# Layer normalisation of four parts placed in the part ahead, piece by piece, in a one-core four-layer network

## The chip, the cores and the metric

The kernel runs on one core of one Trainium2 chip. The metric is the device time of one execution in microseconds (us). Five engines matter: TensorE (PE in the rows; PEld is its loading of weights), VectorE (DVE), ScalarE (ACT), GpSimd (POOL) and SyncE (SP), which here only issues DMA. A name with a small q behind it, such as SPq, is an engine's instruction queue, where it issues transfers and waits.

## What is computed

A residual network over 2048 tokens of 128 features. Every one of its eight parts sees the layer normalisation of the running sum and adds onto it:

```python
    x = x + _L0_attn_ref(_layernorm(x, axis=-1), ...)   # mamba with its own feed-forward
    x = x + _L0_ffn_ref(_layernorm(x, axis=-1), ...)    # mixture of 8 experts, top 2
    x = x + _L1_attn_ref(_layernorm(x, axis=-1), ...)   # linear attention
    x = x + _L1_ffn_ref(_layernorm(x, axis=-1), ...)    # mixture of 8 experts, top 2, gated
    x = x + _L2_attn_ref(_layernorm(x, axis=-1), ...)   # causal attention with a decay by distance
    x = x + _L2_ffn_ref(_layernorm(x, axis=-1), ...)    # 8 experts of three layers, all computed
    x = x + _L3_attn_ref(_layernorm(x, axis=-1), ...)   # attention in a window of 64 tokens, rotary
    x = x + _L3_ffn_ref(_layernorm(x, axis=-1), ...)    # last feed-forward
```

with

```python
def _layernorm(x, axis=-1, eps=1e-05):
    m = jnp.mean(x, axis=axis, keepdims=True)
    v = jnp.var(x, axis=axis, keepdims=True)
    return (x - m) / jnp.sqrt(v + eps)
```

The decay attention subtracts |i - j| from the score of query i and key j, so far keys vanish:

```python
        scores = jnp.where(causal[None, None], -jnp.inf, scores) + decay[None, None]
        attn = jax.nn.softmax(scores, axis=-1)
        ...
        return out @ Wo.T + bo
```

## The kernel before

The running sum X stays in SBUF as 16 tiles of 128 tokens (T = 16), grouped into 4 chunks of 4 tiles (C = 4, CT = 4, CW = 512 tokens). The parts run one after the other, each a block with a program for each engine; between parts all engines meet. In the order of time they are mamba, experts (moe0), linear attention, experts (moe1), the decay mixer, deep (the eight experts of three layers), the window mixer, and the last feed-forward. Deep, the window mixer and the last feed-forward stand in one block.

Layer normalisation is five pieces, which class Norm (L198 to L251) provides for a chunk or for several at once (a sweep), and functions of class Core (L127 to L192) for linear attention: **stats** on VectorE (mean and variance of every tile, then the variance plus epsilon in veps), **power** on GpSimd (veps to the power of -0.5, in rstd), **rows** on VectorE (X less mean, times rstd, in xn or in rows), **turn** on TensorE (four transposes into a bank of PSUM) and **take** on ScalarE (the bank into xnT, which the projections read). Counting semaphores (ln_ve, ln_rs, ln_xn, ln_tr, ln_ev) order them across all parts.

The order of the work on each engine is the order in which it is written. Both mixers are one function, softmax_mixer (L2244). Its loop runs over y from FIRST = -2 to T + 1, with eight steps w = 0 to 7 in each (a step is two heads of sixteen); at one y TensorE makes the scores of tile y + 2 for the maxima (first_pass), those of tile y for the weights (second_pass), and the values, while VectorE takes the maxima of tile y + 2 (L2549) and adds the finished tile y - 2 onto X (add, L2623, at w = 1). GpSimd splits the queries and keys of the tiles from 2 on into parts of 16 bits (split, lines L2778 to L2785) and, in the decay mixer, computes their lengths (L2559 to L2566). There, X plus the output bias stands in a tile of its own, X0, written by one instruction:

```python
                if y == 4 and not windowed:
                    nc.gpsimd.tensor_tensor(X0[:], k.X[:], bo[:, None, :].to_broadcast([P, T, P]), ALU.add)\
                        .then_inc(s_x0, 1)
```

The decay mixer looks only at keys in a band near the query. A block behind it (from L2735) takes the largest lengths and computes a flag that says whether the band is enough; if not, all_keys computes the attention again over all keys from X0. With the data of this kernel the flag says that it is.

In the experts, each tile of 128 routed tokens is fetched by a gather and its answer scattered; the tail (both, onto_x, L1580 to L1588) adds both answers of a token and adds them onto X, chunk by chunk as the transfers land. Deep (L1769) has 32 units, an expert and a chunk each; a step n of its loop holds first(n), second(n - 1) and the third layer of n - 2, and in its first steps the turn and the gate of a chunk. The last feed-forward brings its own normalisation into the window mixer's loop by the tables TURNS, STATS, ROWS and TAKES, whose keys are (y, w).

Of the kernel before, what the change touches and what calls it, by code (L numbers as in the profile page):

```python
# [33 lines left out]
P = 128  # L34
# [8 lines left out]
class Core:  # L43
# [82 lines left out]

    def norm_stats(self, h, X=None):  # L127
        v = self.nc.vector
        X = self.X if X is None else X
        tiles, done = self.sweeps[h], self.Q + h + 1  # L130
        for i in tiles:
            last = v.bn_stats(self.stats[:, i, :], X[:, i, :])
        last.then_inc(self.ln_st, 1)
        self.wait_alone(v, self.ln_st, done)
        for i in tiles:
            last = v.bn_aggr(self.meanvar[:, i, :], self.stats[:, i, :])
        last.then_inc(self.ln_mv, 1)
        v.wait_ge(self.ln_mv, done)
        part = slice(tiles[0], tiles[-1] + 1)
        v.tensor_scalar(self.veps[:, part], self.meanvar[:, part, 1], EPS, None, ALU.add).then_inc(self.ln_ve, 1)  # L140

    def norm_rows(self, L0, c, X=None, keep=None):
        v = self.nc.vector
        X = self.X if X is None else X
        if c < 2:
            v.wait_ge(self.ln_rs, self.Q + c + 1)
        if L0 + c >= 2 and keep is None:
            v.wait_ge(self.ln_tr, L0 + c - 1)
        for i in range(CT):
            n = c * CT + i  # L150
            dst = self.xn[:, (L0 + c) % 2, i, :] if keep is None else keep[:, n, 0:P]
            last = v.tensor_scalar(dst, X[:, n, :], self.meanvar[:, n, 0:1],
                                   self.rstd[:, n:n + 1], ALU.subtract, ALU.mult)
        last.then_inc(self.ln_xn, 1)

    def norm_vector(self, L0, X=None, keep=None):
        for h in range(len(self.sweeps)):
            self.norm_stats(h, X)
        for c in range(self.C):
            self.norm_rows(L0, c, X, keep)  # L160

    def norm_pow(self, h):
        tiles = self.sweeps[h]
        part = slice(tiles[0], tiles[-1] + 1)
        self.nc.gpsimd.tensor_tensor(self.rstd[:, part], self.veps[:, part], self.mhalf[:, part], ALU.pow)\
            .then_inc(self.ln_rs, 1)

    def norm_pool(self):

        for h in range(len(self.sweeps)):  # L170
# [3154 lines left out]
```

## Time and profile before

| what | value |
|---|---|
| median of 3 runs | 1403.57 us (1401.08 to 1407.66) |
| profiled execution | 1401.1 us, span 1399.4 us |
| mean granted clock of TensorE | 0.909 |
| TensorE busy | 1105.9 us, 79% |
| VectorE busy | 892.5 us, 64% |
| ScalarE busy | 680.1 us, 49% |
| GpSimd busy | 573.1 us, 41% |
| instructions | 25149 |

The time is that of the whole execution; the span runs from the profile's first to its last instruction. The parts lie about so in the span: mamba to 344 us, experts to 497, linear attention to 538, experts to 724, decay mixer to 930, deep to 1055, window mixer to 1239, last feed-forward to the end. The granted clock is TensorE's, as a share of 2.4 GHz; 0.50 is 1.2 GHz. A profile holds one execution, and its time stands 2.5 us under the median of the runs.

### The profile page before, as it was taken

How to read it: one execution, taken by the hardware profiler on the slowest of the kernel's cores; microseconds unless marked ns; L12 is line 12 of the kernel's file. 1: busy time of each engine (PE TensorE's matmuls, PEld its weight loads, DVE VectorE, ACT ScalarE, POOL GpSimd, SP SyncE). 2: the span in 40 equal slices, each digit the busy share in tenths (PEclk: the TensorE clock that was granted, in tenths of full speed). 3: DMA queues.
4: the chain of work that ended last, by engine and by line, in shares of the span. 5: the costliest groups of instructions: out<-in, count | busy, mean ns of one | idle time of the engine just before them, and what ended most of it. 6: DMA issues, size and time to landing. Idle time of an engine off the chain costs nothing. (4 is left out here: it accounts for less than half of the span.)

```text
span 1399.4 us, 25149 instructions
## 1 busy us (share of the span) xinstructions
PE 1105.9 (79%) x8340; PEld 714.4 (51%) x8349; DVE 892.5 (64%) x2981; ACT 680.1 (49%) x1256; POOL 573.1 (41%) x739
## 2 busy tenths in 40 slices
PE   8876777679278644299936999859995999899998
PEld 3322222227178633199934777634333777654545
DVE  3599899995545456377549888743858778850200
ACT  2685466545134301132216888627664888641221
POOL 6188889882734414544435434120013655110000
PEclk9989999999589955599968999979996999999999
DMA  2999000000522215311120000020002000000000
GB/s 61 161 191 167 0 0 1 0 0 9 182 61 58 69 38 206 70 42 46 33 72 1 2 3 3 2 57 1 1 0 85 3 3 2 3 1 0 15 0 15
DMA packets 80456, 58.31 MB, mean 42 GB/s; under 512 B 14043, under 2 KB 69221, under 8 KB 80326
## 3 DMA queue, kind: packets, MB, share of 16 engines
q1 hardware_dynamic: 74630, 45.20, 15.3%
q0 software_dynamic: 4544, 9.38, 1.8%
q10 hardware_dynamic: 1152, 2.10, 0.4%
q8 instruction: 70, 1.15, 0.3%
q14 instruction: 60, 0.49, 0.1%
HBM read 28.13 MB, written 28.52 MB: 40 GB/s over the span
## 5 line engine op out<-in xcount | busy, mean ns | idle before, releaser
L713 PE MATMUL bank<-hC,ident 128*128 128x512 f32 x256 | 132.7, 643 | 48.7 <-POOL hC L998 46.7
L998 POOL TENSOR_TENSOR hC<-h,Cs 128x1024 f32<-128x1024 f32 x64 | 150.8, 2356 | 49.8 <-DVE h L897 49.5
L897 DVE TENSOR_TENSOR_SCAN h<-bank,state,dBx 128x512 f32<-128x512 f32 x128 | 157.3, 1270 | 3.7 <-POOL dBx L991 1.7
L1381 POOL DMA_INDIRECT moe_answers<-moe_yw,moe_xg x78 | 84.3, 1081 | 128.6 <-DVE moe_yw L1558 69.7
L2549 DVE CUSTOM_DVE_ANT_0 decay_below<-bank,decay_q_mask 128x256 bf16<-128x256 f32 x256 | 97.2, 419 | 23.0 <-PE bank L2361 22.1
L713 PEld LDWEIGHTS bank<-hC,ident 128*128 128x128 f32 x256 | 46.0, 197 | 111.2 <-POOL hC L998 71.8
L2549 DVE CUSTOM_DVE_ANT_0 window_below<-bank,window_q_mask 128x192 bf16<-128x192 f32 x256 | 80.4, 353 | 29.5 <-PE bank L2361 27.9
L810 ACT ACTIVATE bank<-dt,A 128x512 f32<-128x512 f32 x128 | 83.2, 683 | 28.1 <-DVE h L897 27.1
L1452 PE MATMUL bank<-moe_xgT,moe_wac 128*128 128x128 f32 x624 | 87.4, 286 | 6.5 <-issue 4.1
L2489 ACT ACTIVATE decay_pb<-bank 128x512 f32<-128x512 f32 x128 | 76.2, 598 | 33.3 <-PE bank L2376 32.7
L1467 PE MATMUL bank<-moe_wd,moe_hT 128*128 x624 | 83.0, 277 | 5.7 <-DVE moe_hT L1545 2.7
L1452 PEld LDWEIGHTS bank<-moe_xgT,moe_wac 128*128 128x128 f32 x624 | 80.4, 202 | 7.4 <-issue 4.5
L1467 PEld LDWEIGHTS bank<-moe_wd,moe_hT 128*128 128x128 f32 x624 | 76.4, 194 | 6.5 <-issue 6.4
L2489 ACT ACTIVATE window_pb<-bank 128x384 f32<-128x384 f32 x128 | 62.3, 491 | 34.3 <-PE bank L2376 32.4
L3174 DVE TENSOR_TENSOR f_ys<-bank,f_s 128x256 f32<-128x256 f32 x8 | 3.4, 424 | 117.4 <-PE bank L3117 117.4
L1254 POOL DMA_INDIRECT moe_slots<-moe_rows,moe_slot x64 | 62.3, 973 | 31.7 <-issue 16.6
L226 POOL TENSOR_TENSOR rstd<-veps,mhalf 128x4 f32<-128x4 f32 (+1 forms) x12 | 14.8, 1237 | 145.9 <-DVE veps L220 145.9
L1394 ACT ACTIVATE moe_xgT<-bank 128x128 f32<-128x128 f32 x78 | 20.9, 268 | 97.4 <-PE bank L1445 97.4
L883 DVE TENSOR_TENSOR dBx<-dtx,bank 128x768 f32<-128x768 f32 (+1 forms) x64 | 65.9, 1030 | 1.7 <-ACT taps_w L815 1.3
L832 ACT ACTIVATE Cs<-bank 128x512 f32<-128x512 f32 x64 | 38.1, 596 | 44.2 <-POOL hC L998 35.9
L1445 PE MATMUL bank<-ident,moe_xg 128*128 128x128 f32 x78 | 22.6, 290 | 42.5 <-DMA moe_xg<-moe_slots 41.6
L3108 PE MATMUL bank<-f_hB,f_h2w 128*128 128x512 f32 x128 | 55.3, 592 | 0.0
(480 smaller groups left out, 2834.2 us busy)
## 6 DMA issues: line engine op xcount, KB each, us to landing
moe_slots<-blank SPq DMA_DIRECT2D x16, 1040.0 KB, 17.6
moe_xg<-moe_slots SPq DMA_DIRECT2D x78, 65.0 KB, 1.9
moe_wa<-in_moe_w SPq DMA_DIRECT2D x2, 2048.0 KB, 9.5
moe_back<-moe_answers SPq DMA_DIRECT2D x8, 256.0 KB, 5.6
moe_back<-moe_answers ACTq DMA_DIRECT2D x8, 256.0 KB, 5.7
moe_wu<-in_moe_wu SPq DMA_DIRECT2D x1, 2048.0 KB
deep_w<-in_deep_w SPq DMA_DIRECT2D x3, 512.0 KB
moe_answers<-moe_yw,moe_xg POOLq DMA_INDIRECT x78, 2.5
```

The lines of the kernel that those rows point to most:

```text
L713: last = nc.tensor.matmul(sum_bank(hh)[:], k.ident[:], hC[:, u % 2, hh, :], start=(n == 0), stop=(n == NS - 1))
L810: nc.scalar.activation(decay_bank(u, hh)[:], dt[:, hh, cols(c)], ACT.Exp, scale=A[:, hh, n:n + 1]).then_inc(q_dA, 1)
L883: v.tensor_tensor(dBx[:, u % 2, :, 0:w], dtx[:, :, c * CW:c * CW + w], b_bank[:, None, 0:w].to_broadcast([P, H, w]), ALU.mult).then_inc(q_ ...
L897: v.tensor_tensor_scan(h[:, u % 2, hh, :], decay_bank(u, hh)[:], dBx[:, u % 2, hh, :], state[:, n, hh:hh + 1], ALU.mult, ALU.add).then_inc ...
L998: g.tensor_tensor(hC[:, u % 2], h[:, u % 2], Cs[:, u % 2, None, :].to_broadcast([P, H, CW]), ALU.mult).then_inc(q_hC, 1)
L1254: k.nc.gpsimd.indirect_dma_start(k.slots[self.name], index, self.rows[j][:, i, :], None)\
L1381: nc.gpsimd.indirect_dma_start(answers, bass.IndirectOffsetOnAxis(index, 0), yw[:, i % NY, :], None)\
L1452: last = nc.tensor.matmul(bank[1 + i % 2][:, f * P:(f + 1) * P], wac[:, i % 2, f * P:(f + 1) * P], xgT[:, i % 2, :], start=True, stop=True)
L1467: last = nc.tensor.matmul(bank[6 + i % 2][:, 0:P], hT[:, i % NH, f, :], wd[:, one, f, :].rearrange("p o d -> p (o d)"), start=(f == 0), st ...
L2489: nc.scalar.activation(pb[:, w % 4, :], bank[2 + w % 2][:, 0:2 * HW], ACT.Exp).then_inc(s_ex, 1)
L2549: last = nc.vector.tensor_tensor_reduce(out=below[:, 2 * g + j, :], in0=bank[g % 2][:, j * HW:(j + 1) * HW], in1=q_mask[:], scale=-1.0, sc ...
L3108: last = k.nc.tensor.matmul(bank[4 + m % 4][:], self.hw[layer][:, i, f * P:(f + 1) * P], src[:, i, :], start=(i == 0), stop=(i == FB - 1))
```

## The change

It has six parts.

1. Norm serves linear attention as well, and the functions of Core go. There each chunk is a sweep of its own. Chunk 0's stats and power stand in the tail of the experts ahead (moe0).
2. In the decay mixer the sweeps are now (0), (1), (2, 3) where they were (0), (1, 2, 3). All five pieces of chunk 0 stand in the tail of moe1. stats(1) stands ahead of the loop, the stats of the sweep (2, 3) behind the maxima of (y, w) = (-2, 7), rows of chunk 2 at (-1, 3) and of chunk 3 at (0, 3). The window mixer has the same tables and sweeps, and its own chunk 0 where it was.
3. The normalisation of chunks 0 to 2 of deep stands in the decay mixer's loop, by the tables of the new class NormAhead, which also serves the last feed-forward, in new steps. Deep turns and normalises only chunk 3, computes three gates first, and waits for its weights one layer at a time. The turned rows of deep lie in another buffer (blank).
4. X0 becomes a copy of X, made at y = 6, and X gets the output bias in place by the instruction behind it. add reads X.
5. The check of the band stands in the decay mixer's loop, at y = 12 and 13, in place of the block behind it. The branch for all keys normalises again what it needs.
6. The table of tile ends in the experts is one scan in place of a copy and seven adds.

```diff
+class NormAhead:
+
+    STATS = {(11, 2): 0, (12, 2): 1, (14, 2): 2}
+    ROWS = {(13, 2): 0, (15, 2): 1, (15, 3): 2}
+    TURNS = {(14, 2): 0, (15, 4): 1, (16, 0): 2}
+    TAKES = {(14, 4): 0, (15, 6): 1, (16, 0): 2}
...
+    def vector_step(self, dve, y, w):
+        if (y, w) in self.STATS:
+            dve.wait_ge(self.added, (self.STATS[y, w] + 1) * CT)
+            self.norm.stats(dve, self.STATS[y, w])
+        if (y, w) in self.ROWS:
+            self.norm.rows(dve, self.ROWS[y, w])
+
+    def pool_end(self, pool):
+        for c in range(self.k.C - 1):
+            self.norm.power(pool, c)
...
@@ experts
-                step(v.tensor_copy(ends[:, 0:1], tiles[:, 0:1]))
-                for e in range(1, E):
-                    step(v.tensor_tensor(ends[:, e:e + 1], ends[:, e - 1:e], tiles[:, e:e + 1], ALU.add))
+                step(v.tensor_tensor_scan(ends[:], k.ones[:, 0:E], tiles[:], 0.0, ALU.mult, ALU.add))
...
                 both(0)
-                for c in range(C):
-                    if c + 1 < C:
-                        both(c + 1)
-                    onto_x(c)
+                onto_x(0)
+                dve.wait_ge(s_x, 1)
+                after.stats(dve, 0)
+                both(1)
+                onto_x(1)
+                if full:
+                    after.rows(dve, 0)
+                both(2)
+                both(3)
+                onto_x(2)
+                onto_x(3)
...
@@ linear
-                k.norm_vector(L0, keep=rows)
+                for c in range(C):
+                    norm.rows(dve, c, keep=rows)
+                    if c + 1 < C:
+                        norm.stats(dve, c + 1)
...
@@ deep, tensor
-            turn(0)
+            for c in range(C - 1):
+                gate(c)
             for n in range(STEPS):
                 if n < units:
                     first(n)
-                if n + 1 < C:
-                    turn(n + 1)
-                if 0 <= n - 1 < C:
-                    gate(n - 1)
+                if n == 0:
+                    turn(C - 1)
+                if n == 1:
+                    gate(C - 1)
...
@@ deep, scalar
-            take_turned(0)
-            act.wait_ge(w_1, 32)
-            act.wait_ge(w_2, 32)
-            act.wait_ge(w_3, 32)
+            for c in range(C - 1):
+                take_logits(c)
             for n in range(STEPS):
+                if n == 0:
+                    act.wait_ge(w_1, 32)
                 if n < units:
                     relu_first(n)
...
@@ softmax_mixer
+        FLAG_AT = T - 3
...
+        TURN_AT = {-2: 1, 0: 2, 1: 3}
+        ROWS_AT = {(-1, 3): 2, (0, 3): 3}
...
         def add(dve, y):
             dve.wait_ge(s_pr, y + 1)
-            base = k.X if windowed else X0
             if y == 0 and not windowed:
-                dve.wait_ge(s_x0, 1)
-            nc.vector.tensor_tensor(k.X[:, y, :], bank[7][:, P:2 * P], base[:, y, :], ALU.add).then_inc(s_x, 1)
+                dve.wait_ge(s_x0, 2)
+            nc.vector.tensor_tensor(k.X[:, y, :], bank[7][:, P:2 * P], k.X[:, y, :], ALU.add).then_inc(s_x, 1)
...
@@ vector
+            m.ready(dve)
             if not windowed:
-                for c in range(C):
-                    vector_head(dve, c)
-            m.ready(dve)
+                norm.stats(dve, 1)
...
-                if 1 <= y + 4 < C:
-                    norm.rows(dve, y + 4)
...
+                    if (y, w) == (FIRST, G - 1):
+                        norm.stats(dve, 2)
+                    if (y, w) in ROWS_AT:
+                        norm.rows(dve, ROWS_AT[y, w])
...
+                    if not windowed and (y, w) == (FLAG_AT - 1, 7):
+                        band_is_enough(dve, 0)
+                    if not windowed and y == FLAG_AT and w >= 4:
+                        band_is_enough(dve, w - 3)
...
@@ gpsimd
+            norm.power(pool, 1)
             for y in range(OWN, T):
+                if y == 4:
+                    norm.power(pool, 2)
...
-                if y == 4 and not windowed:
-                    nc.gpsimd.tensor_tensor(X0[:], k.X[:], bo[:, None, :].to_broadcast([P, T, P]), ALU.add)\
+                if y == 6 and not windowed:
+                    pool.wait_ge(k.ln_xn, norm.L0 + C)
+                    nc.gpsimd.tensor_copy(X0[:], k.X[:]).then_inc(s_x0, 1)
+                    pool.wait_ge(s_x0, 1)
+                    nc.gpsimd.tensor_tensor(k.X[:], k.X[:], bo[:, None, :].to_broadcast([P, T, P]), ALU.add)\
                         .then_inc(s_x0, 1)
...
@@ LastFeedForward
-    TURNS = {(15, 2): 0, (15, 5): 1, (16, 0): 2}
-    STATS = {(14, 0): 0, (14, 3): 1, (14, 6): 2}
-    ROWS = {(15, 0): 0, (15, 3): 1, (15, 6): 2}
-    TAKES = {(15, 3): 0, (15, 6): 1, (16, 0): 2}
```

GpSimd in the decay mixer before: decay_left, decay_qp and decay_kp are of the split of a tile, decay_square and decay_norm of the lengths of the tile ahead of it, and decay_X is X0. First the place behind y = 4:

```order
L2559 TENSOR_TENSOR decay_square<-decay_raw 128x256
L2561 TENSOR_TENSOR decay_square<-decay_square 128x32x4
L2563 TENSOR_TENSOR decay_square<-decay_square 128x32x2
L2566 TENSOR_TENSOR decay_norm<-decay_square 128x32
L2716 TENSOR_TENSOR decay_X<-X,decay_bo 128x2048
L2784 TENSOR_TENSOR decay_left<-decay_raw,decay_qp 128x128
L2785 TENSOR_TENSOR decay_left<-decay_raw,decay_kp 128x128
```

And GpSimd of the changed kernel, behind the split and the lengths of y = 6:

```order
L2600 TENSOR_TENSOR decay_square<-decay_square 128x32x4
L2602 TENSOR_TENSOR decay_square<-decay_square 128x32x2
L2605 TENSOR_TENSOR decay_norm<-decay_square 128x32
L2781 COPY decay_X<-X 128x2048
L2783 TENSOR_TENSOR X<-X,decay_bo 128x2048
L2829 TENSOR_TENSOR decay_left<-decay_raw,decay_qp 128x128
L2830 TENSOR_TENSOR decay_left<-decay_raw,decay_kp 128x128
```

One instruction has become two, and they have moved two turns of GpSimd's loop back.

TensorE at the start of deep before: L245 is turn, L1884 a first layer, L1859 a gate, L1891 a second layer.

```order
L245 MATMUL bank<-ident,xn 128x128 x4
L1884 MATMUL bank<-xnT,deep_w 128x512
L245 MATMUL bank<-ident,xn 128x128 x4
L1884 MATMUL bank<-xnT,deep_w 128x512
L245 MATMUL bank<-ident,xn 128x128 x4
L1859 MATMUL bank<-xnT,deep_gw 8x512
L1891 MATMUL bank<-deep_h,deep_w 128x512
L1884 MATMUL bank<-xnT,deep_w 128x512
```

The same place in the changed kernel, where L1877 is a gate, L1902 a first layer, L177 turn, L1909 a second and L1917 a third layer:

```order
L1877 MATMUL bank<-blank,deep_gw 8x512 x3
L1902 MATMUL bank<-blank,deep_w 128x512
L177 MATMUL bank<-ident,xn 128x128 x4
L1902 MATMUL bank<-blank,deep_w 128x512
L1877 MATMUL bank<-blank,deep_gw 8x512
L1909 MATMUL bank<-deep_h,deep_w 128x512
L1902 MATMUL bank<-blank,deep_w 128x512
```

Three gates stand ahead of the first layer, and three of the four turns are gone from here.

VectorE at the end of the decay loop's first y before, with a maximum in L2549 and the rows of chunk 3 in L235:

```order
L2549 ISA decay_below,decay_mx<-bank,decay_q_mask 128x256
L2549 ISA decay_mx 128x1
L235 TENSOR_SCALAR xn<-X,meanvar,rstd 128x128 x4
L2549 ISA decay_below,decay_mx<-bank,decay_q_mask 128x256
L2549 ISA decay_mx 128x1
```

The same place in the changed kernel, with the maximum in L2588:

```order
L2588 ISA decay_below,decay_mx<-bank,decay_q_mask 128x256
L2588 ISA decay_mx 128x1
L142 BN_STATS stats<-X 128x6 x8
L146 BN_AGGR meanvar<-stats 128x2 x8
L150 TENSOR_SCALAR veps<-meanvar 128x8
L2588 ISA decay_below,decay_mx<-bank,decay_q_mask 128x256
```

The statistics of eight tiles stand where the rows of chunk 3 stood; the rows of chunks 2 and 3 each follow later in the loop.

## Rows read from the trace of the kernel before

**Rows 1.** Stretches: length, busy us of PE, PEld, DVE, ACT, POOL, clock, DMA.

```profile
724.00:930.00 206.00, 174.81 (x2468) 130.44 (x2468) 159.60 (x776) 145.34 (x245) 73.99 (x179) 0.94 0.01 2
750.00:760.00 10.00, 6.52 (x63) 4.42 (x63) 9.81 (x53) 6.29 (x10) 6.07 (x17) 1.00 0.00 1
780.00:800.00 20.00, 19.55 (x302) 15.06 (x301) 16.59 (x82) 16.76 (x29) 8.01 (x23) 1.00 0.01 3
...
1078.00:1084.00 6.00, 3.62 (x35) 2.52 (x35) 5.97 (x37) 3.77 (x7) 3.93 (x11) 1.00 0.00 0
946.00:948.00 2.00, 2.00 (x3) 0.77 (x3) 0.47 (x1) 0.68 (x1) 0.00 (x0) 0.52 0.00 0
1048.00:1051.00 3.00, 0.00 (x0) 0.00 (x0) 2.87 (x5) 0.11 (x1) 0.00 (x0) 0.89 0.00 0
```

**Rows 2.** Timeline of the decay mixer's start: start, length, instruction, idle before and releaser.

```profile
724.48 0.87 DVE L212 BATCH_NORM_STATS2 stats<-X 128x6 f32<-128x128 f32 x4 [1.09 <-PEq L117]
...
727.24 1.11 DVE L235 TENSOR_SCALAR xn<-X,meanvar,rstd 128x128 f32<-128x128 f32 x4 [1.17 <-POOL rstd L226]
728.27 2.41 DVE L212 BATCH_NORM_STATS2 stats<-X 128x6 f32<-128x128 f32 x12
...
730.47 4.21 PE L2319 MATMUL bank<-decay_wqkv,xnT 128*128 128x384 f32 x6 [0.77 <-ACT xnT L251]
...
732.26 0.56 DVE L2542 TENSOR_TENSOR decay_raw<-bank,decay_bqkv 128x384 f32<-128x384 f32 x1 [0.32 <-PE bank L2319]
```

**Rows 3.** Timeline of linear attention, VectorE.

```profile
496.63 0.29 DVE L132 BATCH_NORM_STATS2 stats<-X 128x6 f32<-128x128 f32 x1 [1.12 <-PEq L117]
...
504.27 3.17 DVE L152 TENSOR_SCALAR lin_rows<-X,meanvar,rstd 128x128 f32<-128x128 f32 x12 [1.39 <-POOL rstd L165]
```

**Rows 4.** Timeline of the first routing table: the adds and the last scatter.

```profile
374.02 1.32 DVE L1515 TENSOR_TENSOR moe_ends<-moe_ends,moe_tiles 128x1 f32<-128x1 f32 x7
...
388.05 0.96 POOL L1254 DMA_INDIRECT moe_slots<-moe_rows,moe_slot  x1 [0.30 <-issue]
```

**Rows 5.** Timeline around X0, the casts of L2590, and a large GpSimd write.

```profile
760.95 4.52 POOL L2716 TENSOR_TENSOR decay_X<-X,decay_bo 128x2048 f32<-128x2048 f32 x1
...
762.00 3.52 DVE L2590 CAST decay_mp<-decay_mleft 128x16 bf16<-128x16 f32 x1
...
781.53 0.28 DVE L2623 TENSOR_TENSOR X<-bank,decay_X 128x128 f32<-128x128 f32 x1
...
783.39 0.24 POOL L2566 TENSOR_TENSOR decay_norm<-decay_square 128x32 f32<-128x32 f32 x1
...
L2590 DVE CAST decay_mp<-decay_mleft x16: 191/195/3524, 753.2 to 906.2; 128x16 bf16<-128x16 f32 x16
...
L445 POOL MEMSET blank<- 128x2080 f32 x1 | 1.8, 1832 | 0.0
```

**Rows 6.** Timeline from the end of the decay mixer to deep's sixth unit.

```profile
924.24 0.29 DVE L2623 TENSOR_TENSOR X<-bank,decay_X 128x128 f32<-128x128 f32 x1 [0.60 <-PE bank L2409]
...
926.95 0.14 DVE L2745 CAST decay_flag<-decay_both 1x1 uint32<-1x1 f32 x1
...
929.86 0.35 SPq L1829 DMA_DIRECT2D deep_gw<-in_deep_gate_w  x1
...
940.83 0.69 ACT L1961 ACTIVATE deep_h<-bank,deep_c 128x512 f32<-128x512 f32 x1 [4.91 <-DMA deep_c<-in_deep_b]
...
942.05 2.07 PE L1884 MATMUL bank<-xnT,deep_w 128*128 128x512 f32 x2 [3.10 <-ACT xnT L251]
...
944.91 1.88 PE L1859 MATMUL bank<-xnT,deep_gw 128*8 128x512 f32 x2
...
959.88 1.02 PE L1884 MATMUL bank<-xnT,deep_w 128*128 128x512 f32 x2
```

**Rows 7.** Timeline of the window mixer: GpSimd's rotation of step 4, TensorE near the end.

```profile
1085.86 1.48 POOL L2635 TENSOR_TENSOR window_rot<-window_raw,window_cs 128x128 f32<-128x128 f32 x4 [0.36 <-ACT window_raw L2453]
...
1231.05 0.49 PE L2409 MATMUL bank<-window_wo,window_onT 128*128 128x128 f32 x2 [0.80 <-DVE window_onT L2616]
```

More of the change, by code:

```diff
@@ L142, in norm_rows @@
[L142 to L170, printed above, removed]
-            self.nc.gpsimd.wait_ge(self.ln_ve, self.Q + h + 1)
-            self.norm_pow(h)
@@ new lines, in normalise_again, with _ @@
+def normalise_again(k, name, X, to, chunks):
+    a = Again(k, X, to, lambda n: k.sem(f"{name}_{n}"))
+    norm = Norm(a, tuple((c,) for c in range(chunks)))
+    with k.nc.Block() as block:
+        @block.gpsimd
+        def _(pool):
+            for c in range(chunks):
+                norm.power(pool, c)
+        @block.tensor
+        def _(pe):
+            for c in range(chunks):
+                norm.turn(pe, c, k.bank[7])
+        @block.scalar
+        def _(act):
+            for c in range(chunks):
+                norm.take(act, c, k.bank[7])
+        @block.vector
+        def _(dve):
+            for c in range(chunks):
+                norm.stats(dve, c)
+            for c in range(chunks):
+                norm.rows(dve, c)
@@ L1255, in scatter, with experts @@
                     .then_inc(self.s_sent, 16)
-def experts(k, r, early, first):
+def experts(k, r, early, after, full, first):
     nc, t, C, T, E = k.nc, k.t, k.C, k.T, k.E
@@ L1382, in _ @@
                         .then_inc(s_out[i % NY], 16)
+                after.power(pool, 0)
             @block.scalar
@@ L1428, in _ @@
                 fetch_answers(act, 1)
+                if full:
+                    after.take(act, 0, bank[7])
             @block.tensor
@@ L1483, in _ @@
                         down(i - 1)
+                if full:
+                    after.turn(pe, 0, bank[7])
             @block.vector
@@ L1635, in _ @@
             def _(pool):
+                for c in range(1, C):
+                    norm.power(pool, c)
                 nc.gpsimd.memset(half[:], -0.5).then_inc(s_h, 1)
-                k.norm_pool()
                 pool.wait_ge(s_h, 1)
@@ L1654, in _ @@
                 for c in range(C):
-                    k.norm_tensor(L0 + c, kept=rows[:, c * CT:(c + 1) * CT, :])
+                    norm.turn(pe, c, bank[6 + c % 2], keep=rows, behind=1)
                     for i in range(c * CT, (c + 1) * CT):
@@ L2409, in project, with longest_of_all, tensor @@
             nc.tensor.matmul(bank[7][:, P:2 * P], onT[:], wo[:], start=True, stop=True).then_inc(s_pr, 1)
-        def tensor(pe):
+        def longest_of_all(pe):
+            pe.wait_ge(s_f, 1)
+            pe.wait_ge(s_qT, T)
+            for a in range(2):
+                last = nc.tensor.matmul(bank[6][0:1, a * P:(a + 1) * P], small[:, a:a + 1], k.ident[:], start=True, stop=True)
+            last.then_inc(s_f, 1)
+        def tensor(pe, head=True):
             m.ready(pe)
-            norm.turn(pe, 0, bank[7])
+            if head:
+                norm.turn(pe, 0, bank[7])
             for y in range(EARLY):
@@ L3063, in gpsimd @@
     def gpsimd(self, pool):
-        for c in range(self.k.C):
-            self.norm.power(pool, c)
+        self.norm.power(pool, self.k.C - 1)
     def pair(self, pe, n):
```

223 lines of the change are left out of this document (106 added, 117 removed).

## The prediction

> **What bounds the kernel now.** I read the page's busy shares first, then the table of stretches, then the timeline of each place that the diff touches. TensorE is busy 174.8 of the decay mixer's 206 us, VectorE 159.6, and such sums hide two regimes. In the steady loop TensorE works 19.55 of 20 us and VectorE 16.59, so TensorE sets the time and each 10 us hold about 1.7 us of slack on VectorE. At the loop's start it is the other way round: VectorE works 9.81 of 10 us, TensorE 6.52, and in the window mixer 5.97 of 6 against 3.62 [rows 1]. So a piece of normalisation on VectorE costs next to nothing in the steady loop, its full length at a loop's start, and its full length again between two parts, where TensorE waits for it. The change moves pieces among these three places; each is costed on its own.
>
> **Linear attention and the tail ahead of it.** The statistics of chunk 0 go into the tail of the first mixture of experts, and in linear attention the other three chunks are now served one after the other: statistics, power on GpSimd, rows. Start of statistics to start of rows is 727.24 - 724.48 = 2.76 us, a chunk's rows 728.27 - 727.24 = 1.03 [rows 2]. Three rounds are 3 x 3.79 = 11.4 us, with the first rows 12.4. Started at 496.6, plus 0.6 for the longer tail, they end at 509.6, where the twelve rows of before ended at 504.27 + 3.17 = 507.4 [rows 3]. TensorE used to work off a backlog of chunks behind that, and now has only one; I take half of the 2.2 us and write **+1.2** (0 to +2.2).
>
> **Scan.** Seven adds of 1.32 us become one instruction, twice. Behind them the table of tile ends hurries for nothing: the first gather waits for the last of the scatters, which GpSimd issues one after another until 388.05 + 0.96, 13.7 us after the adds [rows 4]. That queue hides it: **0** (were the cover gone, -1.2 twice).
>
> **Start of the decay mixer.** Statistics, power, rows, turn and copy of chunk 0 move into the experts' tail: 1.6 us of statistics (724.48 to 727.24 - 1.17, where the wait for the power begins) and 1.0 of rows, of which some lie in gaps between the DMA answers: +1.8. What goes are the 6.0 us from 724.48 to the first multiplication at 730.47: it can start as the part is entered, and the first addition of a bias, 1.8 us behind it, hides chunk 1's statistics, which now stand ahead of it. Against that the statistics of chunks 2 and 3 (eight of the twelve tiles that take from 728.27 to 731.94, so 2.4 us) and the rows of chunk 2 (1.0) now stand among the first maxima, where VectorE is full: +3.4, less 0.1 for waits there [rows 1, 2]. 1.8 - 6.0 + 3.3 = **-0.9** (-3 to +0.9).
>
> **X0, two effects.** Before, one GpSimd addition over 128x2048 starts at 760.95 and takes 4.52 us. Beside it a cast of 16 elements on VectorE starts at 762.00, takes 3.52 us and ends with the addition; the sixteen casts of that line have a median of 195 ns [rows 5]. It lies in the VectorE-bound stretch, so 3.3 us are lost to it. The change takes the addition from there: **-3.3** (0, if the loop makes it up, to -3.3). The Trainium skill, "GPSIMD Engine Reference", section 1 (Specifications), says that GpSimd shares its SBUF interfaces with VectorE, with contention for instructions in a 2-port mode or with two SBUF inputs; the trace agrees with it in that the cast, from SBUF to SBUF, stood for as long as the addition ran.
>
> At its new place two operations stand in a row, behind the lengths that end at 783.39 + 0.24 = 783.63: a copy of X, then the addition in place. The first residual addition on VectorE (781.53 before) now needs the second of them. The trace has no GpSimd copy of this size: writing 128x2080 alone takes 1.83 us, reading two operands and adding 4.52 [rows 5]. I take 1.9, as a copy is nearer to the first, with 4.5 as upper bound. X is ready at 783.63 + 1.9 + 0.1 + 4.5 = 790.1, so the addition is 8.6 us late. VectorE's maxima stand behind it and TensorE's passes behind these; 1.7 us of slack go off, so TensorE stands for about 7 us. After such a pause its granted clock falls: with TensorE idle from 1048 it averages 0.89 over 3 us, so the fall comes near the end of them, and a return took from 942.05 to about 947.9 of steady work (0.52 over 946 to 948) [rows 1, 6]. Five us at 1.2 instead of 2.4 GHz lose 2.5. Together **+9.5** (7, without the clock, to 12.1 with a copy of 4.5). In a sentence of its own: the Trainium skill, "GPSIMD Engine Reference", section 3.1, has a body of 1.03 cycles for an element with up to two operations, which for 2048 elements is an estimated 1.8 us, and its 4497 ns for an addition of this size agrees with the 4.52 here.
>
> **Inside the decay loop.** Three statistics of 1.6 us, three rows of 1.0, three turns on TensorE, the check's two small multiplications and five short VectorE operations. VectorE's slack takes most of its part. A turn moves 512 columns, at most half of a gate's 1.88, 0.94 us at full clock [rows 6]; I take 0.6 for it and 0.5 for the check, 2.3 in all, and TensorE has only 0.45 free in 20: **+2.0** (+1 to +4).
>
> **The check's block.** From the end of the last residual addition, 924.53, to the first load of the next part are 5.3 us, of which the check's own chain is about half; it runs to 927.09 [rows 6]. Without it the next part begins 2.56 earlier: **-2.6** (-2 to -2.6).
>
> **Start of deep.** Three of four chunks are normalised already. Before, counted from the first load at 929.86, the sixth unit's first layer started at 959.88, +30.0. Now three gates come first, each of 1.9 us on TensorE at half clock with a copy of 0.7 behind it for which the next one waits; with the gate's small load there at +2.6 (chosen, no row has it) they end at about +10.0. Then first(0) and a turn, 944.91 - 942.05 = 2.9, to +12.9. The clock rises after the 5.9 us of work that it took before, at +15.9. A unit at full clock is 2.5: from 942.05 to 959.88 are 17.8 us, 14.9 with the 5.9 counted half, less two turns and four gates, for four units. The second unit has two layers and a gate, 5.3 at half clock, of which 3.0 lie before the rise and the rest is 1.2; three more are 7.5. That gives +24.6: **-5.4**. Were the clock up at +8.5, because the gates count as such work, it is +21.2 and -8.8. ScalarE's wait for the biases (4.91, to 940.83, which is +11.0) is no hindrance, since first(0) ends at +12 [rows 6]; a later landing gives the other end, -3.
>
> **Window mixer.** Its start loses as that of decay does, and gains less, since the twelve tiles' statistics are not ahead of the first multiplication. Eight tiles' statistics (2.4) and the rows of chunk 2 (1.0) come into the full stretch; the power for them stands in GpSimd's queue ahead of the rotation of step 4, which before started at 1085.86 with 0.36 us to spare [rows 7], so it is free too late, and VectorE probably waits another 1 to 2 us for it; one rows of 1.0 goes away: **+3.5** (+1 to +5.5). In its last steps statistics come at a better place: TensorE waited 0.80 us for a VectorE copy that stood behind one [rows 7], and the other two cost 0.3 elsewhere: **-0.5** (-1 to +0.5).
>
> **Sum.** 1.2 + 0 - 0.9 - 3.3 + 9.5 + 2.0 - 2.6 - 5.4 + 3.5 - 0.5 = **+3.5 us**. The profiled execution took 1401.1 (span 1399.4), so 1404.6 for one like it; the median of the three runs is 1403.57, which makes 1407.1. Below 7.0 us (0.5%) no difference can be told from none, so the forecast is no change that can be measured.
>
> **Rivals.** *Slower:* the pair on GpSimd is longer than I take it. With a copy as dear as the addition, 4.5 us, +9.5 becomes +12.1; with no slack on VectorE either, since the normalisation and the lost start have eaten it, +13.8. The sum is then 7.8, the time 1411.4. It decides from a copy of about 3.7 us with that slack gone. For it: every other GpSimd operation here that reads and writes is dearer than a write alone. Against: the write of 2080 elements in 1.83.
>
> *Faster:* the gates of deep bring the clock up early (-8.8 for -5.4) and the pause at X0 is too short to lose it (7.0 for 9.5), with the window's start at its lower bound (+1 for +3.5). The sum is 3.5 - 8.4 = -4.9, the time 1398.7; only with the loop's +2.0 and the 1.2 of linear attention absorbed too is it 1395.5 and past the bound. For it: the gates keep TensorE at work two thirds of the time. Against: with 3 of 4 us idle it had no such clock.
>
> *The pieces are hidden:* what moves ahead of deep and decay only turns their wait into one for weights or masks. Then the two starts give nothing (+0.9 and +5.4) and the time is 1413.4. Against it: the loads that deep's first unit needs had landed by 940.83, one microsecond before it would need them.
>
> *By the shared interface:* the pair at its new place stops VectorE's work in SBUF again. VectorE is held by the residual addition then, so this costs nothing, or 3.3 us if its instructions are still running: 1410.4. The rule is the Trainium skill's, "GPSIMD Engine Reference", section 1.
>
> **How the numbers follow.** The forecast 0.52, slower by the pair 0.14, faster 0.16, hidden pieces 0.10, second collision 0.08. The bounds of the terms give the likeliest case 1401 to 1413 of its own; the range is 1397 to 1414. Faster by over 0.5%: 0.14, mostly of the faster case; slower: 0.24, of the slower ones and the forecast's upper edge; within 0.5%: 0.62.
>
> **What would show it.** On VectorE one long wait for GpSimd at the first residual addition of decay, 8 to 9 us, beside a TensorE gap of about 7 and a granted clock of 0.5 behind it; if that wait is missing, 9.5 us of my sum is wrong and the kernel is faster. No cast of 3.5 us in the decay loop. Linear attention about 1 us longer; the time from decay's last residual addition to deep 2.6 shorter; deep's sixth unit at +24 to +25. In the window mixer, a wait of VectorE for the reciprocal roots ahead of its third rows.

## The result: 0.6% slower

| | before | changed |
|---|---|---|
| median | 1402.58 us (7 runs, 1401.08 to 1407.66) | 1412.37 us (7 runs, 1407.88 to 1414.10) |
| profiled execution | 1401.1, span 1399.4 | 1409.7, span 1408.0 |

The ratio over all runs is 1.0057, 95% interval 1.0037 to 1.0076, so the change costs 5 to 11 us. The forecast of 1407.1 us was 5 us too low. The time lies in the stated range of 1397 to 1414 us, near its upper end, and the loss is clear of zero, so "no measurable difference" did not hold.

Both kernels issue nearly the same TensorE instructions in the same order, so each instruction can be looked up in both timelines. The shift of such pairs, changed less before, tells where the time went. Start times in us:

```
instruction on TensorE                 before   changed   shift   since the row above
down of the first experts              467.49    467.73   +0.24
end of linear attention                535.57    539.39   +3.82   +3.6   linear attention and its border
down of the second experts             704.63    708.59   +3.96   +0.1   the experts with the scan
decay loop, y = 1                      762.43    767.76   +5.33   +1.4   border and start of the mixer
decay loop, y = 3                      782.18    786.60   +4.42   -0.9   X0 no longer at y = 4
decay loop, after X0                   790.50    804.22  +13.72   +9.3   X0 at y = 6
last of the decay loop                 922.99    937.94  +14.95   +1.2   pieces inside the loop
deep, sixth unit, first layer          959.88    965.54   +5.66   -9.3   check, border, start of deep
window loop, y = 2                    1109.63   1118.46   +8.83   +3.2   start of the window mixer
window loop, y = 14                   1223.68   1233.04   +9.36   +0.5   pieces inside the loop
last feed-forward                     1256.47   1264.05   +7.58   -1.8   last steps of the window mixer
```

The largest single term is as forecast. The timeline of the changed kernel around X0, GpSimd, VectorE and TensorE, and the table of stretches behind it:

```profile
788.01 1.89 POOL L2781 COPY decay_X<-X 128x2048 f32<-128x2048 f32 x1
789.98 4.50 POOL L2783 TENSOR_TENSOR X<-X,decay_bo 128x2048 f32<-128x2048 f32 x1
...
794.58 0.29 DVE L2661 TENSOR_TENSOR X<-bank,X 128x128 f32<-128x128 f32 x1 [8.50 <-POOL X L2783]
...
795.61 0.61 PE L2389 MATMUL bank<-decay_kT,decay_qT 128*128 128x256 bf16 x2 [6.63 <-DVE decay_mx L2588]
```

```profile
790.00:792.00 2.00, 0.00 (x0) 0.00 (x0) 0.00 (x0) 0.72 (x1) 2.00 (x1) 0.84 0.00 0
792.00:794.00 2.00, 0.00 (x0) 0.00 (x0) 0.00 (x0) 0.00 (x0) 2.00 (x1) 0.50 0.00 0
...
800.00:802.00 2.00, 2.00 (x17) 1.58 (x14) 0.78 (x5) 1.14 (x3) 0.00 (x0) 0.60 0.00 0
802.00:804.00 2.00, 1.89 (x34) 1.36 (x32) 1.97 (x9) 1.10 (x3) 1.48 (x4) 1.00 0.04 8
```

The copy takes 1.89 us, the residual addition is 8.5 us late, TensorE stands for 6.6, its clock (the last but two of the numbers) falls to 0.50 at the end of 790 to 792 and is back near 801.6. These 9.3 us are more than the whole shift of 7.5.

What the forecast did not have stands at the two borders behind the experts. VectorE's first instructions of linear attention and of the decay mixer, in the timeline:

```profile
500.60 0.35 DVE L166 TENSOR_SCALAR lin_rows<-X,meanvar,rstd 128x128 f32<-128x128 f32 x1 [4.42 <-PEq L117]
...
732.65 0.87 DVE L142 BATCH_NORM_STATS2 stats<-X 128x6 f32<-128x128 f32 x4 [3.48 <-PEq L117]
```

Before, these waits were 1.12 us [rows 3] and 1.09 us [rows 2]. L117 is the meeting of all engines in end_part, so the row says only that somebody came late. Who it was stands in the instructions of the block's own line, which an engine issues when it leaves a block. Those of the changed kernel (number, then shortest, median and longest in ns, first and last start):

```profile
L1345 PEldq DRAIN  x2: 805/982/1160, 479.3 to 726.8; - x2
L1345 POOLq DRAIN  x2: 7011/7172/7332, 492.5 to 724.2; - x2
...
L1345 DVEq DRAIN  x2: 1202/1203/1204, 495.0 to 728.0; - x2
```

and the same line of the kernel before:

```profile
L1340 POOLq DRAIN  x2: 8291/8449/8607, 480.8 to 708.8; - x2
...
L1340 DVEq DRAIN  x2: 1202/1203/1204, 494.4 to 722.2; - x2
```

Here are GpSimd's last instruction ahead of the first border before, and the one of the changed kernel, from the timelines:

```profile
482.89 0.96 POOL L1381 DMA_INDIRECT moe_answers<-moe_yw,moe_xg  x1 [0.30 <-issue]
```

```profile
492.54 1.41 POOL L156 TENSOR_TENSOR rstd<-veps,mhalf 128x4 f32<-128x4 f32 x1 [8.45 <-DVE veps L150]
```

GpSimd's drain is recorded with 7 to 8.6 us, and the record begins while GpSimd's last instructions still run. Before, it began at 480.8, the last scatter ended at 483.85, and the drain was over at 489.4, while VectorE still added the answers. Now the power of chunk 0 stands in that queue and ends at 493.95: the drain ends at 499.5, and all engines wait. Counted from the end of GpSimd's last instruction, both drains take 5.5 us; at the second border both take 5.9.

Last, the starts of deep and of the window mixer. Timeline, the residual addition that ends the decay mixer, deep's first statistics, gates and layers, and VectorE's wait in the window mixer:

```profile
939.18 0.29 DVE L2661 TENSOR_TENSOR X<-bank,X 128x128 f32<-128x128 f32 x1 [0.58 <-PE bank L2437]
942.85 0.87 DVE L142 BATCH_NORM_STATS2 stats<-X 128x6 f32<-128x128 f32 x4 [3.39 <-PEq L117]
...
944.65 1.88 PE L1877 MATMUL bank<-blank,deep_gw 128*8 128x512 f32 x2 [5.51 <-DMA deep_gb<-in_deep_gate_b]
951.97 2.08 PE L1902 MATMUL bank<-blank,deep_w 128*128 128x512 f32 x2
...
955.90 1.02 PE L1877 MATMUL bank<-blank,deep_gw 128*8 128x512 f32 x2
...
965.54 1.02 PE L1902 MATMUL bank<-blank,deep_w 128*128 128x512 f32 x2
...
1092.29 1.49 DVE L166 TENSOR_SCALAR xn<-X,meanvar,rstd 128x128 f32<-128x128 f32 x4 [2.03 <-POOL rstd L156]
```

From the last residual addition's end to deep's first statistics are now 3.4 us. Before, from 924.53 [rows 6] to the statistics at 929.90, they were 5.4. The fourth gate takes 1.02 where the first three took 1.88: the clock is 0.50 until 955 and 0.90 over 955 to 956, so it rises at about 955.2. That is 10.6 us behind the start of the first gate, 12.4 behind the first load (942.81), and 3.5 us sooner than I had it. The wait for the power ahead of the window mixer's third rows is 2.0 us.

### The profile page after: what moved, and what is told of

It reads as the page before. It is cut to its first block and busy times, and to the rows that moved or that the text cites. A ratio compares the mean times of both kernels' runs of the same rounds, so it can differ in the third digit from the quotient of the medians.

```text
span 1408.0 us, 25143 instructions
## 1 busy us (share of the span) xinstructions
PE 1109.2 (79%) x8340; PEld 715.5 (51%) x8349; DVE 885.8 (63%) x2971; ACT 680.6 (48%) x1256; POOL 576.1 (41%) x744
## 5 line engine op out<-in xcount | busy, mean ns | idle before, releaser
L2588 DVE CUSTOM_DVE_ANT_0 decay_below<-bank,decay_q_mask 128x256 bf16<-128x256 f32 x256 | 97.3, 419 | 23.1 <-PE bank L2389 22.3
L2588 DVE CUSTOM_DVE_ANT_0 window_below<-bank,window_q_mask 128x192 bf16<-128x192 f32 x256 | 80.0, 353 | 26.0 <-PE bank L2389 24.5
L156 POOL TENSOR_TENSOR rstd<-veps,mhalf 128x4 f32<-128x4 f32 (+1 forms) x18 | 20.3, 1129 | 147.9 <-DVE veps L150 147.9
L2389 PE MATMUL bank<-decay_kT,decay_qT 128*128 128x256 bf16 x256 | 51.1, 286 | 12.6 <-DVE decay_mx L2588 12.4
```

The source lines that it names most:

```text
L2389: last = nc.tensor.matmul(both[:, :, a:b], qT[:, y % 3, g, :], kT[:, (y - 1 + s) % R, g, :, P - (b - a):P], start=(s == 0), stop=(s == 1), ...
L2588: last = nc.vector.tensor_tensor_reduce(out=below[:, 2 * g + j, :], in0=bank[g % 2][:, j * HW:(j + 1) * HW], in1=q_mask[:], scale=-1.0, sc ...
```

## The experiments

Ten kernels. Every one is compared with the kernel before on its own chip where a time is given, and by shifts of the same TensorE instructions where a term is given. A single run's time is given with that of before beside it and settles nothing by itself; e1, e3, e5, e6, e7 and e9 are single runs.

**e1: the power out of the tail** of the first experts.

```diff
-                after.power(pool, 0)
+                if full:
+                    after.power(pool, 0)
...
-                for c in range(1, C):
+                for c in range(C):
                     norm.power(pool, c)
```

> The changed kernel with one instruction moved: the power of chunk 0 leaves GpSimd's queue at the end of the first experts and stands at the head of linear attention's. Theory A (GpSimd's drain at the end of the experts, 7.0 us, starts only behind that power): the wait of VectorE at the border, 4.4 us, goes back to the 1.1 us of the kernel before, VectorE then waits about 1 us for the power, and linear attention ends 2 to 2.5 us earlier. Theory B (the border is late for another reason, such as the statistics in the tail or more code behind it): the wait at the border stays above 4 us, and linear attention is no earlier or 1 us later. In both the second border (3.5 us) is unchanged.

VectorE's waits in the timeline of this kernel:

```profile
494.58 0.07 DVE L1716 MEMSET lin_rows<- 128x16 f32 x1 [1.14 <-PEq L117]
495.61 1.11 DVE L166 TENSOR_SCALAR lin_rows<-X,meanvar,rstd 128x128 f32<-128x128 f32 x4 [0.95 <-POOL rstd L156]
```

The border is back at 1.14 us, and linear attention ends 2.2 us earlier against the changed kernel (the shift of its instructions goes from -2.78 to -4.99). Theory A. The second border still waits 3.48 us, as both theories had it. Its time was 1405.12, before 1401.61.

**e9: the drain by itself**, in the kernel before: a GpSimd memset of one column behind the last scatter, which waits for chunk 0 of X. It adds work that the reference does not need and leaves nothing out.

```diff
+                pool.wait_ge(s_x, 1)
+                nc.gpsimd.memset(late[:], 0.0)
```

> The kernel before with one instruction more in each experts part: a GpSimd memset of one column at the end of its queue, which waits for chunk 0's addition onto X. No normalisation is moved. Theory A (GpSimd's drain takes 5 to 6 us behind whatever GpSimd does last there, and was hidden because GpSimd finished early): both borders come 1.5 to 3 us later, VectorE's waits there are 3 to 4 us in place of 1.1, and the time rises by 3 to 5 us. Theory B (the drain is long only behind the scatters themselves, and short behind anything later): both borders stay at 1.1 us.

The memset and the drains in this kernel, from the timeline and from the block's line:

```profile
490.91 0.10 POOL L1385 MEMSET moe_late<- 128x1 f32 x1 [8.47 <-DVE X L1590]
...
721.95 0.10 POOL L1385 MEMSET moe_late<- 128x1 f32 x1 [8.91 <-DVE X L1590]
```

```profile
L1341 POOLq DRAIN  x2: 5657/5818/5979, 490.9 to 721.9; - x2
```

Both borders come 2.7 us later (-1.43 to +1.30, and +1.75 to +4.48), with VectorE waiting 3.40 and 3.71 us. A memset of 0.1 us with no normalisation moved costs 5.4 us in the trace; the time was 1404.96, before 1398.43. Theory A holds: the drain ends 5.5 us behind the memset at the first border and 5.9 at the second, the same as behind a scatter or a power, although here the last scatter had been issued 8.5 us before the memset. What it does in that time no record shows. GpSimd's drain is short where the block has few or no gathers and scatters (1.1 us in linear attention with none, 2.6 in mamba's block with 4, against 67 and 71 in the two mixtures), but no run changes their number.

**e6: linear attention in one sweep**, on top of e1.

```diff
-        lin_norm = Norm(k, ((0,), (1,), (2,), (3,)))
+        lin_norm = Norm(k, ((0,), (1, 2, 3)))
...
-                for c in range(C):
-                    norm.rows(dve, c, keep=rows)
-                    if c + 1 < C:
-                        norm.stats(dve, c + 1)
+                norm.stats(dve, 1)
+                for c in range(C):
+                    norm.rows(dve, c, keep=rows)
```

> The kernel of the first experiment (power out of the experts' tail) with chunks 1 to 3 of linear attention in one sweep of statistics ahead of all rows. Theory A (three round trips of statistics, power and rows cost 1.2 us or more against one): linear attention ends 2 to 2.5 us earlier than in that kernel, 4.3 to 4.8 earlier than in the changed one and about 1 earlier than before. Theory B (the first rows are what counts, since TensorE is the slower one behind them): no earlier than in that kernel.

Counted against the experts ahead of it, the first turn starts 2.6 us later than in e1, the last 3.3 earlier, and linear attention ends 4.4 earlier, 2.9 earlier than before. That is the direction of theory A, and more than it said. Its size cannot be told from this run: the clock rose at 503.2 here and at 499.5 in e1, and of e8 and e10 below, which have the same program in this part, one ends it level with before and the other 2.9 us ahead. So of linear attention's +3.6 us, 2.2 are shown to be the drain. The other 1.4 remain in e1, and how much of them the round trips are stays open. The time of e6 was 1400.81, before 1398.43.

**e7: the decay mixer's start as before**, in the changed kernel: no piece in the tail, sweeps (0) and (1, 2, 3), rows at the old places.

```diff
-            experts(k, routing, decay, decay_norm, True, first=0)
+            experts(k, routing, decay, None, False, first=0)
...
-            if not windowed:
-                norm.stats(dve, 1)
+            if not windowed:
+                for c in range(C):
+                    vector_head(dve, c)
```

> The changed kernel with the whole normalisation of the decay mixer as before: nothing of it in the experts' tail, all of it at the mixer's start. Theory A (by my sum, the moved pieces gain 0.9 us): 0.9 us slower at y = 2 of that loop. Theory B (the drain behind the power in the tail took 2.4 us, so the piece loses): the border is back at 1.1 us, and the loop's y = 2 is 0.5 us or more earlier than in the changed kernel; the rest of the trace is the same.

At the first multiplication of the mixer the shift is unchanged (from -1.6 in the experts to 0.0, 1.6 later: the head is longer), and at y = 2 it is -3.4. So the moved pieces lost 1.8 us there, where I had them gain 0.9: they brought the first multiplication forward by 1.6 us and not by the 4.2 (6.0 less 1.8) of my sum, and then cost 3.4 for my 3.3. A further 0.6 came back behind X0. Theory B. Time 1404.21, before 1398.43.

**e5: the window mixer's start as before**, in the changed kernel, by the same edits for that mixer.

```diff
-        window_norm = Norm(k, ((0,), (1,), (2, 3)))
+        window_norm = Norm(k, ((0,), (1, 2, 3)))
...
+                if OLD and 1 <= y + 4 < C:
+                    norm.rows(dve, y + 4)
```

> The changed kernel with the start of the window mixer's normalisation as before: statistics of chunks 1 to 3 in one sweep ahead of the loop, rows of chunk 2 ahead of it, of chunk 3 after its first y. Theory A (eight tiles' statistics, a rows and the wait of 2.0 us for GpSimd's power stand where VectorE bounds the loop, 3.2 us in all): TensorE's work from 1097 us on comes 3.0 to 3.3 us earlier than in the changed kernel, the wait is gone, and the time is about 1409. Theory B (the late start of GpSimd's rotation, or the clock that falls there, made the loss by itself): less than 2 us come back.

The shift goes from +2.7 to -0.5: 3.2 us, to a tenth what the changed kernel had lost. Theory A. The time was 1408.22, before 1398.43.

**e3: the window mixer's later pieces inside the loop**, in the changed kernel: statistics of eight tiles at (1, 1), rows at (2, 0) and (3, 0), turns and copies at (2, 5) and (3, 5).

```diff
-        ROWS_AT = {(-1, 3): 2, (0, 3): 3}
+        ROWS_AT = {(2, 0): 2, (3, 0): 3} if windowed else {(-1, 3): 2, (0, 3): 3}
+        STATS_AT = (1, 1) if windowed else (FIRST, G - 1)
+        POWER_AT = 6 if windowed else 4
+        LATE_TURN = {(2, 5): 2, (3, 5): 3} if windowed else {}
```

> The changed kernel with statistics, power, rows, turn and copy of chunks 2 and 3 moved in the window mixer alone from its first steps to y = 1 to 3. Theory A (VectorE bounds the first steps and TensorE the later ones, so that a piece costs its length only at the start): the drift of 3.2 us between 1085 and 1097 goes away, and 2 to 3 us of it stay away. Theory B (the pieces cost the same wherever they stand, or the wait for GpSimd's power was the whole of it): at most 2 us come back.

Neither theory. 4.6 us come back by 1098, but all of it is lost again by 1142, and at the end this kernel is 1.1 us later than the changed one (shift +0.6 ahead of the mixer, +1.7 behind it). The time was 1411.36, before 1401.61. Timelines of VectorE and TensorE at the statistics, and the stretch behind them:

```profile
1104.45 1.63 DVE L142 BATCH_NORM_STATS2 stats<-X 128x6 f32<-128x128 f32 x8
1106.22 0.64 DVE L146 BATCH_NORM_AGGREGATE meanvar<-stats 128x2 f32<-128x6 f32 x8
...
1108.42 0.54 PE L2422 MATMUL bank<-window_pb,window_V 128*32 128x128 f32 x16 [2.10 <-issue]
```

```profile
1110.00:1111.00 1.00, 1.00 (x10) 0.77 (x8) 0.26 (x2) 0.36 (x1) 0.56 (x2) 0.50 0.00 0
```

A piece of 2.6 us stops TensorE for 2.1, in a stretch where TensorE sets the time, and behind the stop its clock is 0.50 from 1109.4 to 1112.8. Together the shift grows by 3.7 us there; the rows and turns take the rest. The slack on VectorE is there, but in small parts between two pairs of heads, because the program has two banks of scores for TensorE to run ahead in. The changed kernel's pieces in the decay loop are shorter, three statistics of 1.6 us and three rows of 1.0, and with the turns and the check they cost 1.2 us together. No run tries the short pieces in the window mixer.

**e2: the X0 pair one turn earlier**, in the changed kernel.

```diff
-                if y == 6 and not windowed:
+                if y == 5 and not windowed:
```

> The changed kernel with the copy X0 and the in-place addition one turn earlier in GpSimd's loop, at y = 5. Theory A (the 9.3 us are the pair being late): the pair ends before the first residual addition wants it, VectorE's wait of 8.5 us and TensorE's of 6.6 are gone, and the time falls by 8.5 to 9.5 us, to about 1403. Theory B (the pair costs wherever it stands, through the shared interface): a VectorE cast or two-operand instruction of 3 to 5 us appears beside it and 3 us or more of the gain is lost.

1402.45 us, the median of ten runs (1400.85 to 1420.33), before 1401.61; the ratio is 1.0032 (1.0003 to 1.0060), from 1.0057. The two intervals overlap, and this one holds the single run of 1420.33, so the size of the gain is read from the traces: there 7.6 of the 9.3 us come back; the waits of 8.5 and 6.6 are gone. VectorE and TensorE in this kernel:

```profile
778.55 4.53 POOL L2783 TENSOR_TENSOR X<-X,decay_bo 128x2048 f32<-128x2048 f32 x1
...
781.23 1.90 DVE L2609 TENSOR_TENSOR decay_norm2max<-decay_norm,decay_norm2max 128x32 f32<-128x32 f32 x1
...
784.20 0.49 PE L2437 MATMUL bank<-decay_wo,decay_onT 128*128 128x128 f32 x2 [1.96 <-DVE decay_onT L2655]
```

An addition of 32 columns takes 1.90 us and ends with GpSimd's, at 783.1, and TensorE waits 1.96 for what stands behind it: the missing 1.7. So both theories have their part, A the larger. The Trainium skill, "GPSIMD Engine Reference", section 1 (Specifications), names VectorE instructions with two SBUF inputs as one of the two kinds that contend; this one has two. The copy ahead of it held up nothing, but no VectorE instruction with all its operands in SBUF ran beside it.

**e4: the same shift of X0 in the kernel before**, from y = 4 to y = 5.

> The kernel before with one edit: its GpSimd addition X0 stands at y = 5 and not at y = 4. Theory A (my term: the 3.5 us cast beside it costs 3.3 us because VectorE bounds that stretch): the time falls by 2.5 to 3.3 us, with the long cast gone or in a stretch where it costs nothing. Theory B (the loop makes up for the cast): within 1 us of before, though the cast of 3.5 us is gone from 762.

1398.60 us, before 1401.61, ratio 0.9982 (0.9972 to 0.9993), so 1.0 to 3.9 us faster. In the two traces the old place gave back 1.35 us and the new one took 0.2; another 1.2 us lie at the start of deep, which the edit does not touch. No VectorE instruction took over 0.7 us beside the addition. So the cast of 3.5 us had cost about 1.3, not 3.3: between the two theories, nearer to B. The trace of the kernel before shows the same on TensorE, in its timeline:

```profile
765.59 0.62 PE L2344 MATMUL bank<-identb,decay_mp 128*128 128x128 bf16 x8 [1.31 <-DVE decay_mp L2590]
```

While the cast stood, TensorE still had scores and values to do until 764.3, and then waited 1.31 us for it.

**e8 and e10: what the runs favour, together.** The changed kernel with the starts of both mixers as before (e5, e7), linear attention as in e6 and the X0 pair at y = 5. e10 has it at y = 4.

> The changed kernel with what the runs so far favour: the X0 pair at y = 5, the starts of the decay and of the window mixer as before, linear attention with chunk 0's statistics in the tail ahead, its power at its own start, and one sweep for the rest. Kept of the change: deep's normalisation and the band check in the decay loop, the new steps for the last feed-forward, the scan. If the effects add, against the kernel before: linear -0.9, X0's old place -1.3 and its new one +1.7, the decay loop +1.2, border, check and start of deep -8.3, the window mixer's last steps -1.3: -8.9 us in all, about 1392 to 1394, ratio 0.993 to 0.995. If they don't add (theory B: a gain at deep's start only returned what the loops before had lost), it is within 4 us of before.

> The combined kernel with the X0 pair at y = 4, where the addition of before stood. Theory A (GpSimd's addition holds up the first VectorE instruction with its operands in SBUF that meets it, and this costs more in the VectorE-bound stretch): one VectorE instruction of 2 to 5 us between 760 and 772, and 0 to 2 us slower than with y = 5. Theory B: no difference.

e8: 1394.87 us, ratio 0.9922 (0.9901 to 0.9942). e10: 1391.66 us, ratio 0.9902 (0.9884 to 0.9921). Before was 1406.06 on that chip. Both beat both kernels by these ratios. For e8 that is 8 to 14 us, where effects that add gave 8.9; its trace is 5.7 us shorter than that of before. The intervals of the two overlap; in the traces e10 is 7.0 us ahead, 3.6 of them at X0, where I had it behind, and 3.0 in linear attention, where the kernels are the same and TensorE's clock rose at 504.4 in e10 and at 508.4 in e8. The timeline of e10 at X0, GpSimd and VectorE, and that of e8 with TensorE and the stretch behind it:

```profile
758.54 1.89 POOL L2789 COPY decay_X<-X 128x2048 f32<-128x2048 f32 x1
760.51 4.54 POOL L2791 TENSOR_TENSOR X<-X,decay_bo 128x2048 f32<-128x2048 f32 x1
...
759.63 0.86 DVE L2631 CAST decay_mp<-decay_mleft 128x16 bf16<-128x16 f32 x1
...
764.93 0.18 DVE L2611 TENSOR_TENSOR decay_norm2max<-decay_norm,decay_norm2max 128x32 f32<-128x32 f32 x1
```

```profile
776.12 4.53 POOL L2791 TENSOR_TENSOR X<-X,decay_bo 128x2048 f32<-128x2048 f32 x1
...
778.35 2.35 DVE L2611 TENSOR_TENSOR decay_norm2max<-decay_norm,decay_norm2max 128x32 f32<-128x32 f32 x1
...
781.77 0.80 PE L2439 MATMUL bank<-decay_wo,decay_onT 128*128 128x128 f32 x2 [2.42 <-DVE decay_onT L2657]
```

```profile
782.00:784.00 2.00, 2.00 (x15) 1.75 (x16) 1.26 (x7) 0.60 (x1) 1.65 (x6) 0.50 0.04 8
```

At y = 4 a cast of 0.2 us took 0.86, until the copy ended at about 760.4. Beside the addition VectorE had only maxima and other instructions that read PSUM, none longer than elsewhere, and the addition of 32 columns came at 764.93, as GpSimd's ended, and took 0.18. At y = 5 the same instruction came in the middle of GpSimd's addition and took 2.35, and TensorE's shift grew by 3.6 us against e10: 2.2 by the stop, and 1.4 because the clock fell to 0.50 behind it, until about 784.9. In e2 a stop of 1.96 us was not followed by such a fall. So the engine that bounds the stretch does not tell what the pair costs; which VectorE instruction meets it does, as far as these two traces show.

## Why the prediction was right and wrong

**X0 at y = 6, +9.5: right**, +9.3 with every link as written (copy 1.89 for 1.9, addition 8.5 late for 8.6, TensorE 6.6 for 7, the clock down and back). e2 shows the cause.

**X0 away from y = 4, -3.3: a size.** -0.9 in the changed kernel, -1.35 in e4. The step "it lies in the VectorE-bound stretch, so 3.3 us are lost to it" took a busy row for a bound: TensorE had other work for most of the cast and waited 1.31 us for it.

**Linear attention, +1.2: wrong**, +3.6. The step that failed is "started at 496.6, plus 0.6 for the longer tail": it started at 500.6. The length of the tail on VectorE was counted, GpSimd's drain behind the moved power was not; e1 and e9 show that it is 2.2 to 2.7 us. The other 1.4, against a term of +1.2 (half of 2.2 is 1.1), is no proof of the round trips: the clock in this part moves its end by up to 3.0 us between e8 and e10.

**Start of the decay mixer, -0.9: wrong**, +1.4. "It can start as the part is entered" is what happened, but the part was entered 2.4 us late for the same drain. 2.4 on -0.9 is +1.5. The pieces among the first maxima cost 3.4 us for 3.3 (e7).

**Inside the decay loop, +2.0: a size**, +1.2. **The check, -2.6:** about -2.0; the block is gone, but 3.4 us are left between the parts where 2.8 of the 5.4 were to be. **Start of deep, -5.4: a size**, -7.3. The sixth unit came at +22.7 and not at +24.6, because the first layer came at +9.2 for +10.0 and the clock rose at +12.4 for +15.9. The step that was off is "the clock rises after the 5.9 us of work", counted from the first layer: the third gate at +7.4 ran into that layer without a gap, and the rise came 5.0 us behind its start. It is the faster rival's mechanism, in part (it had the clock up at +8.5); what the first two gates, with gaps behind them, did for it no run shows.

**Window mixer, +3.5 and -0.5:** +3.2 for its start, with the foreseen wait of 2 us, shown by e5. In the loop and its last steps +0.5 and -1.8, so -1.3; no run takes these two apart.

**Scan, 0: right**, 0.1.

**The sum** was +3.5 where the traces have +7.5. The drain, twice 2.3, and the 2.4 us that X0's old place did not give make it 7 us too low; deep and the loop gave back 2.7 of that and the window mixer 1.1, while the check's block gave 0.6 less than I had. So part of the hit is luck: errors of 7 us met errors of 4 with the other sign. None of the rivals named the drain.

## What to carry to other kernels

When a piece is moved into the tail of a block, look at what each engine still has to do to leave it: a queue that ended early can hide a long drain, and an instruction placed late behind it lays the drain open, however small it is. Slack of a helper engine counts only in the pieces in which it comes; a job longer than the buffers between the engines stops the bounding one, though the totals leave room. And before the place of a large GpSimd operation is chosen, look which VectorE instructions with all their operands in SBUF will meet it (two of those held here were casts, with one input), since the place alone made 3.6 us of difference here, 1.4 of it by TensorE's clock behind the stop.

## What the runs showed of the hardware

- GpSimd's drain at the end of the experts' blocks ended 5.5 us (first) and 5.9 us (second) behind the end of GpSimd's last instruction, whether that was a scatter, a power of 1.41 us or a memset of 0.1; in linear attention it took 1.1.
- A GpSimd addition over 128x2048 stretched single VectorE instructions from SBUF to SBUF to 3.5, 1.9 and 2.35 us, each until the addition's own end, where the same ones take 0.2; maxima that read PSUM ran on at 0.42 beside it. A GpSimd copy of the same size (1.89 us) held one cast for 0.66 us in e10; in e2 none met it.
- At deep's start TensorE's clock rose 10.6 us behind the start of three gates of 1.9 us with gaps of 0.9, the last 5.0 us of them without a gap; before, it rose after 5.9 us without one. In or behind stops of 6.63, 2.42 (e8) and 2.10 us (e3) it fell to 0.50, behind one of 1.96 (e2) it did not.
- In linear attention of e8 and e10, with the same instructions, VectorE waited 4.00 and 2.45 us for TensorE and the part ended 3.0 us apart, since the clock rose at different moments. Terms below 3 us next to a cold start of TensorE are not to be read from one profile.
